# Moving the transposes of the embedding duos in TensorE's order: behind a sum batch instead of away from one

## The reference, cut to what matters

```python
e = stack([tbl_f[ids[:, f]] for f in range(40)], axis=1)      # (2048, 40, 64)
z = einsum('bie,fie,bif->bi', e[:, rows], param, e[:, cols])  # (2048, 780)
h = concatenate([z, dense_ctx], axis=1)                       # (2048, 796)
h = maximum(h @ W_top1 + b_top1, 0)                           # 512 wide
h = maximum(h @ W_top2 + b_top2, 0)                           # 256 wide
y = h @ W_top3                                                # (2048, 1)
```

## Time and profile before

| | |
|---|---|
| median of 3 runs | 1202.34 us (1202.31 to 1202.41) |
| span of the profiled execution, first to last instruction | 1200.1 us |
| left around the span, against the median | 2.2 us |
| busy: TensorE, VectorE, ScalarE, GpSimd | 1184.0, 1069.4, 972.4, 633.9 us |
| granted TensorE clock | 0.998 of full speed over the span |

### The profile page before, as it was taken

How to read it: one execution, slowest core, us unless ns; L and a number is a source line. 1 busy time by engine, 2 the same in 40 slices (tenths; PEclk the granted TensorE clock), 3 DMA queues, 4 the chain that set the end, 5 groups by cost and what they waited for, 6 DMA issues and landing times.

```text
span 1200.1 us, 22100 instructions
## 1 busy us (share of the span) xinstructions
PE 1184.0 (99%) x5754; PEld 428.4 (36%) x5754; DVE 1069.4 (89%) x959; ACT 972.4 (81%) x7469; POOL 633.9 (53%) x719
## 2 busy tenths in 40 slices
PE   8989999999999999999999999999999999999999
PEld 3323333333333333333333333333333333333333
DVE  8578999999998889999988888999999989899870
ACT  7448899889788856978997956877898986889992
POOL 6676766556666665655434545566615453007450
PEclk9999999999999999999999999999999999999999
DMA  4224323222222222242222222222313222113200
GB/s 118 52 65 150 78 74 73 70 75 76 68 73 68 64 67 56 69 121 77 71 66 60 57 60 65 66 76 67 75 52 75 61 63 57 45 45 100 69 10 0
DMA packets 51006, 82.13 MB, mean 68 GB/s; under 512 B 13832, under 2 KB 14088, under 8 KB 50496
## 3 DMA queue, kind: packets, MB, share of 16 engines
q1 hardware_dynamic: 31160, 60.48, 16.9%
q0 software_dynamic: 19712, 20.22, 8.6%
q10 hardware_dynamic: 8, 0.01, 0.0%
HBM read 80.65 MB, written 0.01 MB: 67 GB/s over the span
## 4 chain that ended last, share of the span: by engine, by line
PE 97%; ACT 2%; issue 1%; DVE 0%; POOL 0%; POOLq 0%; ACTq 0%
PE ring L787 34%; PE ring L793 28%; PE z_ps L806 17%; PE aux L700 6%; PE aux L750 4%; PE ring L700 2%; PE aux L707 2%; PE aux L740 2%; ACT act_prod L554 1%; PE aux L723 1%; PE aux L714 1%; PE ring L788 1%; PE ring L707 1%; PE ring L794 0%; PE ring L822 0%
## 5 line engine op out<-in xcount | busy, mean ns | idle before, releaser
L554 ACT ACTIVATE act_prod<-act_prod 128x64 f32<-128x64 f32 x3648 | 871.8, 244 | 40.5 <-DVE act_prod L692 39.2
L554 ACT ACTIVATION_READ_ACCUMULATOR act_prod<-act_prod 128x1 f32 x3648 | 696.6, 191 | 0.0
L692 DVE TENSOR_TENSOR prod<-ring,emb 128x1024 f32<-128x1024 f32 x440 | 508.1, 1214 | 46.3 <-PE ring L788 46.0
L487 POOL DMA_INDIRECT stage<-tbl,idx x384 | 362.3, 943 | 297.2 <-issue 155.5
L787 PE MATMUL ring<-emb,raw 64*128 64x512 f32 x880 | 428.4, 610 | 8.4 <-issue 4.3
L788 PE MATMUL ring<-emb,raw 64*128 64x512 f32 x880 | 428.6, 610 | 0.0
L793 PE MATMUL ring<-raw,emb 64*128 64x512 f32 x720 | 365.0, 617 | 2.4 <-issue 1.5
L794 PE MATMUL ring<-raw,emb 64*128 64x512 f32 x720 | 365.1, 618 | 0.0
L692 DVE TENSOR_TENSOR act_prod<-ring,kept 128x1024 f32<-128x1024 f32 x228 | 267.3, 1214 | 38.4 <-PE ring L794 37.7
L487 POOL DMA_INDIRECT kept<-tbl,idx x232 | 219.3, 945 | 135.3 <-issue 105.7
L787 PEld LDWEIGHTS ring<-emb,raw 64*128 64x128 f32 x880 | 151.1, 186 | 230.6 <-issue 139.2
(11 more groups left out here) (57 smaller groups left out, 360.6 us busy)
## 6 DMA issues: line engine op xcount, KB each, us to landing
raw<-param_b SPq DMA_DIRECT2D x200, 256.0 KB
stage<-tbl,idx POOLq DMA_INDIRECT x384
W<-W1g SPq DMA_DIRECT2D x3, 1792.0 KB, 8.8
kept<-tbl,idx POOLq DMA_INDIRECT x232, 2.5
act_prod<-tbl SPq DMA_DIRECT2D x6, 224.0 KB
W<-W2t SPq DMA_DIRECT2D x1, 512.0 KB
idx<-ids_t SPq DMA_DIRECT2D x1, 240.0 KB, 6.1
act_prod<-tbl SPq DMA_DIRECT2D x6, 26.0 KB
```

The costliest lines, as they stand in the source:

```text
L487: pool.indirect_dma_start(to[:, t, E * (f % 2) : E * (f % 2) + E], None, tables[f], bass.IndirectOffsetOnAxis(ap=idx[:, c, f, t : t + 1], ...
L554: op = act.activation(part, part, ACT.Copy, accum_out=sums[:, t, at : at + 1])
L692: dve.tensor_tensor(to, ring[:, n % RING, :, :], by, ALU.mult).then_inc(prod_done, 1)
```

## The change

The shift of a duo now goes to a unit right behind a sum batch, with two more candidates; and a duo gives VectorE room for one reduction.

```diff
-def apart(at):
-    return not any(at - 4 <= x <= at for x in SUM_AT)
+def beside(at):
+    return at - 1 in SUM_AT
...
         if _at < NU * _c + _first[_d] - 4:
-            DUO_AT[_c, _d] = next((_at + u for u in (0, 1, -1, 2, -2, 3) if apart(_at + u)), _at)
+            DUO_AT[_c, _d] = next((_at + u for u in (0, 1, -1, 2, -2, 3, -3, 4) if beside(_at + u)), _at)
...
-ROOM = {"h1": 5, "h2": 3}
+ROOM = {"h1": 5, "h2": 3, "duo": 1}
```

## The result

The changed kernel takes **1254.25 us** (median of 4 runs, 1253.7 to 1254.94) against 1202.32 for the kernel before on the same chip: a ratio of 1.0435, 95% interval 1.0423 to 1.0448. That is 51.9 us more. The forecast was 1246 with a range of 1231 to 1259.

What follows compares the result with a forecast made beforehand. VectorE's fixed work plus its idle time behind TensorE's blocks was taken to decide: 36.0 + 5.6 + 3.2 + 1.9 - 3.2 = +43.5 on 1200.1 gives 1243.6, with 2.2 us around the span 1246; range 1231 to 1259.

Steps and rivals of the forecast that it cites:

- TensorE isn't the bound: Both engines nearly full, tied by a ring of three units; VectorE's idle time, 90 us waiting for TensorE, is lost for good.
- TensorE's saving costed at nothing: At 68 duos joined to sum batches TensorE saves 0.20 us each, 13.7 us, counted as no gain in time.
- +0.585 per uncovered pair: At 39 pairs of sum batch and duo without a reduction, VectorE's gap is a bare batch's plus 0.585 us.
- A reduction covers 1.13 and no more than the gap: In VectorE's gaps one reduction fills 1.13 us, two 2.26; in a pair's gap of 1.37, two waste 0.9.
- lone duos: Three reductions go under duos standing alone in the first 100 us, where VectorE idles anyway: -3.2 us.
- Overlap of products behind idle time, +1.9: A VectorE product after idle time isn't overlapped with the one ahead: 0.08 us each for 23 more gaps, +1.9 us.
- Sum of the batches, +36.0: VectorE's idle time at sum batches, alone or with a duo, rises from 39.5 to 75.5 us.
- wait less: ScalarE's copies, with duos in the third or fourth unit of a batch of four, wait less; costed at nothing.
- TensorE the bound: Rival: TensorE bounds throughout, VectorE has slack, and 68 x 0.20 us comes off: 1188.6 us, chance 0.04.
- the two cancel: Rival: 13.7 us saved on TensorE meets 13.7 us lost in VectorE's longer gaps: 1202 us, chance 0.03.
- Short transposes: Rival: behind a sum batch a duo's four transposes add 0.22 us instead of 0.58: 1232 us, chance 0.04.
- Late copies: Rival: ScalarE copies `aux` late at closely placed turns, four waits up to 4 us, and duo 11: 1266 us, chance 0.05.

Runs made afterwards that it cites:

- e2: Kernel before with its old duo placement, but a duo now gives room for one reduction: 1228.22 us, ratio 1.0212.
- e4: Kernel before with two of the four transposes of each duo, from the fourth duo on, left out: 1197.07 us, ratio 0.9958.
- e3: Changed kernel with two of the four transposes of each duo, from the fourth duo on, left out: 1244.75 us.
- e1: Changed kernel with the new duo placement but the old rooms, a duo giving room for no reduction: 1236.53 us, ratio 1.0283.
- e5: Changed kernel with ScalarE's copies of duos 12 and 17 of the last chunk behind the next batch's reductions: 1481.75 us, 0.9669 of the kernel before there.
- e12: Kernel before, with no reduction under a sum batch if an h1 follows within ten units: 1591.17 us, 0.9996 of the kernel before there.
- e6: Changed kernel with duos 12 and 17 of the last chunk back in their old places: 1490.94 us, 0.9736 of the kernel before there.
- e8: The kernel of e5 again on another chip: 1483.58 us, 0.966 of the kernel before there.
- e9: The kernel of e6 again on another chip: 1489.46 us, 0.9697 of the kernel before there.
- e11: The kernel of e5 once more on another chip: 1516.47 us, 0.954 of the kernel before there.

## Why the prediction was right

- **TensorE isn't the bound.** Right in the main. The chain of 97% was the trap; the 195.35 us of VectorE in 200 was the warning. e2 moves no work of TensorE and loses 26 us; e4 takes 17 us of work from TensorE and gains 5.3.
- **TensorE's saving costed at nothing.** Nearly right. The ring stopped TensorE ahead of 29 of the 39 uncovered pairs, against 15 of the 39 bare batches before. e4 shows that its time had some worth in the kernel before, about 0.3 us per us saved.
- **+0.585 per uncovered pair.** Right: 1.34 at the median against 1.365, and e3 takes 0.22 of it away, pair by pair, by taking 0.22 from the transposes.
- **A reduction covers 1.13 and no more than the gap.** Right: e1 shows 0.21 under one reduction (0.24 expected), e2 the h2 gap up by 1.13, the changed kernel no gap under two. h1 +5.9 against +5.6, h2 +3.2 as priced, lone duos -3.3 against -3.2.
- **Overlap of products behind idle time, +1.9.** Too high: VectorE's busy time grew by 0.6.
- **Sum of the batches, +36.0.** Mis-sized: it measured +45.9. Of the 9.9 us between, 6.9 are the two waits for ScalarE (4.77 and 5.17, against 1.34 and 1.73 without). This is where a step that was put at nothing failed: that ScalarE's copies, with the duos late in a batch of four, "wait less". A later place in a batch does mean that ScalarE has its reductions behind it when it comes to the copy. But then it arrives first and waits: ScalarE's idle time ahead of these copies rose from 65.1 us in 27 cases to

```profile
ACT emb L516 <- PE aux L750: 130.8, 37, 8.1
```

  and what is queued behind the copy waits too. I had looked for copies that come late for TensorE, and not for TensorE coming late for the copies. The other 3 us are spread: the uncovered pairs have 0.7 more (2.17 at the pair of unit 37, which lost its reduction), bare batches without a reduction 1.0 more (1.34 at unit 25, 1.42 at two just behind a y), and those with one reduction, which I had at nothing, 1.2 (1.08 of it at unit 21).
- **The number.** 1254 lies inside the range in part by luck. The 13 us of room above 1246 were kept for longer bare gaps (6), a late copy of duo 11 (4) and no gain in the first part (3). Of these only 3 us of longer gaps came. The rest of what lies above 1246 is the two waits for ScalarE, for which no room was kept; without their 6.9 us the time would be some 1247.
- **The rivals.** "TensorE the bound" and "the two cancel" fell with the first number. Short transposes: the pair shows 0.59, as apart. In the Trainium skill, "TensorE: Matmul & The Clock Gate", section "Back-to-back issue gap", N/2.4 + 2.5 ns is the gap of a single matmul in isolation, an estimated 0.22 us for the four, and the same section has 81 ns per matmul of 128 columns in a stream with weight loads, an estimated 0.32. The traces agree with neither: e3 gives 0.11 us for each fp32 transpose left out, and four between other work take 0.58. Late copies: `aux` was never late for the closely placed turns; duo 11 of chunk 0 was copied at once and cost nothing beyond its pair's gap.

## What to carry to other kernels

When two engines hand work over through a short ring, the chain that ended last can name the one with 97% while, as here, the time is set in the main by the other's idle time behind long blocks. Price each block by the gap that it leaves when the ring is full, count which gaps are filled, and put the filler (here, reductions) one by one where a gap is at least as long as the filler; joining two blocks saves 0.20 us of one excursion but adds their lengths at the one point that has no cover. And when a producer's step is moved later within its batch, look at the in-order queue of the engine that waits for it: what stands behind that wait is late as well.

## What the runs showed of the hardware that I had not expected

On the four chips of e5 to e12 the same kernel before took 1533 to 1589 us instead of 1202. No trace of the kernel before was kept there, but those of its variants were. In the trace of e12 VectorE is busy 1082.0 us and ScalarE 1008.0, against 1069.4 and 972.4 in the kernel before, but they idle in places that wait for nothing the profile shows. ScalarE's and VectorE's waits there:

```profile
ACT act_prod L555 <- issue: 164.6, 309, 8.6
...
DVE act_prod L693 <- remote: 70.2, 19, 7.3
DVE dve_prod L693 <- remote: 66.5, 12, 6.3
```

In the kernel before, where it took 1202 us, neither kind appears for these groups. The first product starts at 101.8 us instead of 29.0, and the next 39 take another 79 us instead of 73. The granted clock was 0.906 over the span, against 0.998, with TensorE busy for 82% of it. And under these conditions the order of the kernels turned: the changed kernel with two duos or their copies moved (e5, e6, e8, e9, e11) was 3 to 5% faster than the kernel before, where the changed kernel is 4.35% slower otherwise. What holds the engines up there, and why the new placement suffers less from it, was not settled. Single gaps of the price list recur in these traces, as at units 696 and 699, but it says nothing about their total times.
